# Small-head attentions on one NeuronCore: stacks of bf16 pieces through DRAM scratch, in whole rows

## What is computed

```python
x = x + _L0_attn_a_ref(_layernorm(x, axis=-1), ...)   # "norm": q and k normalised by head
x = x + _L0_ffn_ref(_layernorm(x, axis=-1), ...)      # six layers of window attention and FFN
x = x + _L0_attn_b_ref(_layernorm(x, axis=-1), ...)   # "latent": causal
x = x + _L0_ffn_ref(_layernorm(x, axis=-1), ...)
x = x + _L1_attn_a_ref(_layernorm(x, axis=-1), ...)   # linear attention
x = x + _L1_ffn_ref(_layernorm(x, axis=-1), ...)
x = x + _L1_attn_b_ref(_layernorm(x, axis=-1), ...)   # "plain": causal
x = x + _L1_ffn_ref(_layernorm(x, axis=-1), ...)

scores = jnp.einsum('bhsk,bhtk->bhst', Q, K) / jnp.sqrt(jnp.asarray(d_k, x.dtype))
scores = jnp.where(causal, scores, -jnp.inf)          # latent and plain
probs = jax.nn.softmax(scores, axis=-1)
attn = jnp.einsum('bhst,bhtk->bhsk', probs, V)
```

## Time and profile before

| | us |
|---|---|
| median of 3 executions | 4672.77 (4668.33 to 4675.03) |
| the profiled execution | 4673.36 |
| its span, first to last instruction | 4671.1 |
| norm attention, about | 65 to 392 |
| latent attention, about | 2100 to 2420 |
| plain attention, about | 4300 to 4620 |
| DVE, ACT, POOL busy | 3373.8, 2957.3, 2325.9 |

### The profile page before, as it was taken

The page is one execution under the profiler, slowest core; times in us unless marked ns, Lnnn a source line. Parts: engine busy times, 40 slices in busy tenths (PEclk is TensorE's granted clock), DMA queues, the critical chain, the costliest instruction groups (busy, mean ns, idle before and its releaser), DMA issues. The chain is left out here.

```text
span 4671.1 us, 129984 instructions
## 1 busy us (share of the span) xinstructions
PE 4231.0 (91%) x54074; PEld 2082.5 (45%) x54074; DVE 3373.8 (72%) x5180; ACT 2957.3 (63%) x7379; POOL 2325.9 (50%) x1448
## 2 busy tenths in 40 slices
PE   5897999999999999976879999999999999877698
PEld 2222555545455554532434545555555555433343
DVE  3673888888888888853648888888888888633463
ACT  2664777777777777752546777777777777643354
POOL 3101766666666666642007666666666666401200
PEclk8997999999999999986999999999999999988799
DMA  5212000000000000003210000000000000000320
GB/s 153 30 22 59 2 20 7 2 20 7 20 7 20 7 2 2 2 4 41 42 37 25 2 20 7 20 7 20 7 3 24 2 2 2 2 4 9 53 31 10
DMA packets 87862, 88.62 MB, mean 19 GB/s; under 512 B 36632, under 2 KB 79860, under 8 KB 83444
## 3 DMA queue, kind: packets, MB, share of 16 engines
q1 hardware_dynamic: 86420, 74.11, 7.7%
q10 hardware_dynamic: 864, 6.29, 0.3%
HBM read 44.13 MB, written 7.34 MB: 11 GB/s over the span
## 5 line engine op out<-in xcount | busy, mean ns | idle before, releaser
L423 POOL TENSOR_TENSOR ra<-ra,rb 128x1024 f32<-128x1024 f32 x384 | 926.9, 2414 | 348.0 <-DVE rb L725 347.9
L437 POOL TENSOR_TENSOR qkr<-ra,inv 128x1024 f32<-128x1024 f32 x384 | 731.0, 1904 | 612.8 <-ACT inv L677 609.1
L467 PE MATMUL ps<-wvo,xs 128*32 128x512 f32 x6144 | 825.1, 609 | 88.1 <-ACT vs L608 67.9
L501 PE MATMUL ps<-wq,xs 128*128 128x512 f32 x1536 | 751.7, 612 | 19.1 <-DMA wq<-in_L_ffn_Wqkv 18.4
L650 ACT ACTIVATE pr<-ps,neg 128x64 f32<-128x64 f32 x3072 | 667.8, 337 | 4.0 <-DVE neg L702 3.9
L608 ACT ACTIVATE vs<-ps 128x512 f32<-128x512 f32 x768 | 450.8, 587 | 251.7 <-PE ps L467 250.7
L1448 DVE TENSOR_REDUCE nm<-ps 128x1 f32<-128x512 f32 (+3 forms) x768 | 382.2, 549 | 244.3 <-PE ps L1257 243.2
L523 PEld LDWEIGHTS ps<-kt,qt 64*32 64x32 f32 x24576 | 359.6, 107 | 293.3 <-issue 289.5
L501 PEld LDWEIGHTS ps<-wq,xs 128*128 128x128 f32 x1536 | 275.0, 192 | 447.4 <-issue 355.9
L725 DVE TENSOR_TENSOR rb<-ps,rope 128x1024 f32<-128x1024 f32 x384 | 465.8, 1213 | 0.0
L722 DVE TENSOR_TENSOR ra<-ps,rope 128x1024 f32<-128x1024 f32 x384 | 451.3, 1175 | 18.6 <-ACT sq L624 11.5
(11 more groups left out here) (229 smaller groups left out, 6439.3 us busy)
## 6 DMA issues: line engine op xcount, KB each, us to landing
qs<-cut SPq DMA_DIRECT2D x216, 64.0 KB
ks<-cut SPq DMA_DIRECT2D x216, 64.0 KB
wq<-in_L_ffn_Wqkv SPq DMA_DIRECT2D x12, 1024.0 KB, 5.3
wvo<-wvo_scratch SPq DMA_DIRECT2D x12, 1024.0 KB, 5.0
wvo_scratch<-pt ACTq DMA_DIRECT2D x6, 1024.0 KB, 4.3
w<-in_L_ffn_W SPq DMA_DIRECT2D x12, 341.0 KB
pt<-in_L_ffn_Wqkv SPq DMA_DIRECT2D x6, 512.0 KB, 8.2
pt<-in_L_ffn_Wo SPq DMA_DIRECT2D x6, 512.0 KB, 7.7
```

Of the source, the lines that this page charges most:

```text
L423: pool.tensor_tensor(ra[:, m % 2, :, :], ra[:, m % 2, :, :], rb[:, :, :], ALU.add).then_inc(sum_done.sem, 1)
L437: pool.tensor_tensor(qkr[:, m % 2, :, :].rearrange("p s (h c) -> p (s h) c", c=HD), ra[:, m % 2, :, :].rearrange("p s (h c) -> p (s h) c", ...
L467: last = pe.matmul(VP[32 * j:32 * j + 32, :], xs[:, turn % 2, v * WIN:v * WIN + WIN], wvo[:, l % 2, j, :], start=True, stop=True)
L501: last = pe.matmul(PJ[:, qk, :], xs[:, turn % 2, t * P:t * P + P], wq[:, l % 2, at:at + 512], start=True, stop=True)
```

## The change

`cut` is no longer copied into the stacks directly. There is a scratch tensor in DRAM per attention, `pieces` (batch, piece, q or k, channel, token). `store_cut` (L1110 of the new kernel) stores each piece as soon as it is split, in three transfers of 256 KB a batch, counted by `cut_stored`. The channels of q and k are now ordered channel first over all 16 heads, so a channel's 16 heads are one contiguous run in `pieces`. `stack` (L1117 for `qs`, L1120 for `ks`) reads 24 rows of a stack at a time. For q they are the 8 channels of one piece, each repeated three times; for k they are the 8 channels of all three pieces. With all heads a row is 16 KB and a transfer 384 KB.

Batch 0 is read in 12 transfers of half the heads, right behind its stores. The other batches are read in 6 transfers, two each at 7, 9 and 11 heads from the start of the batch before, and their stores stand at 1. POOL's split of the next batch waits for `cut_stored` instead of `ld_low` and `ld_high`; `ld_high` is used for batch 0 alone. In the set-up of "norm", `gb` is loaded in 4 transfers instead of 8.

```diff
-    loads = 2 * PARTS * PARTS
+    loads = 2 * PARTS
+    SLOT = PARTS * SD
+    STACK_AT = (7, 9, 11)
+    pieces = nc.dram_tensor(f"{kind}_pieces", (BATCH, PARTS, 2, P, SEQ), BF16, kind="Internal").ap()
...
-                        for e in range(2):
-                            by_row = d[f"{n}_{name}"][:, None].to_broadcast([SD, SH // 2])
-                            sp.dma_start(gb[P // 2 * e:P // 2 * e + P // 2, col:col + 1], by_row, allow_slow_non_contiguous=True).then_inc(ld_w.sem, 16)
+                        by_row = d[f"{n}_{name}"][:, None].to_broadcast([SD, SH])
+                        sp.dma_start(gb[:, col:col + 1], by_row, allow_slow_non_contiguous=True).then_inc(ld_w.sem, 16)
...
-            def stacks(b, low):
-
-                heads = slice(0, SH // 2) if low else slice(SH // 2, SH)
-                half = slice(0, P // 2) if low else slice(P // 2, P)
-                done = ld_low if low else ld_high
-                for part_ in range(PARTS):
-                    sp.wait_ge(cut_done.sem, cut_done.at(5 * b + 2 * part_ + 1))
-                    for to, s, p, c in [(qs, 0, c // PARTS, c) for c in range(PARTS * PARTS)] + [(ks, 1, c % PARTS, c) for c in range(PARTS * PARTS)]:
-                        if p != part_:
-                            continue
-                        rows = slice(SD * c, SD * c + SD)
-                        sp.dma_start(to[rows, b % 2, heads, :], cut[half, p, s, :]).then_inc(done.sem, 16)
+            def store_cut(b, p):
+                sp.wait_ge(cut_done.sem, cut_done.at(5 * b + 2 * p + 1))
+                sp.dma_start(pieces[b, p].rearrange("s r t -> r s t"), cut[:, p, :, :]).then_inc(cut_stored.sem, 16)
+
+            def stack(b, s, p, heads, done):
+
+                rows = (qs, ks)[s][SLOT * p:SLOT * p + SLOT, b % 2, heads, :]
+                if s == 0:
+                    of_part = pieces[b, p, 0].rearrange("(c h) t -> c h t", c=SD)[:, heads, :].rearrange("c h t -> c (h t)")
+                    sp.dma_start(rows, of_part[:, None, :].to_broadcast([SD, PARTS, rows.shape[1] * SEQ])).then_inc(done.sem, 16)
+                else:
+                    all_parts = pieces[b, :, 1].rearrange("e (c h) t -> c e h t", c=SD)[:, :, heads, :].rearrange("c e h t -> c e (h t)")
+                    sp.dma_start(rows, all_parts).then_inc(done.sem, 16)
...
                 if (b := batch_at(k, 1)) is not None:
-                    if b >= 2:
-                        sp.wait_ge(st_mm.sem, st_mm.at(NP * (SH * (b - 2) + SH // 2)))
-                    stacks(b, True)
-                if (b := batch_at(k, 7)) is not None:
-                    if b >= 2:
-                        sp.wait_ge(st_mm.sem, st_mm.at(NP * SH * (b - 1)))
-                    stacks(b, False)
+                    for p in range(PARTS):
+                        store_cut(b, p)
+                    if b == 0:
+                        sp.wait_ge(cut_stored.sem, cut_stored.at(16 * PARTS))
+                        for heads, done in ((slice(0, SH // 2), ld_low), (slice(SH // 2, SH), ld_high)):
+                            for p in range(PARTS):
+                                stack(b, 0, p, heads, done)
+                                stack(b, 1, p, heads, done)
+                for p, at in enumerate(STACK_AT):
+                    if (b := batch_at(k, at)) is not None and b >= 1:
+                        if p == 0:
+                            sp.wait_ge(cut_stored.sem, cut_stored.at(16 * PARTS * (b + 1)))
+                            if b >= 2:
+                                sp.wait_ge(st_mm.sem, st_mm.at(NP * SH * (b - 1)))
+                        stack(b, 0, p, slice(0, SH), ld_low)
+                        stack(b, 1, p, slice(0, SH), ld_low)
...
                     if b:
-                        pool.wait_ge(ld_low.sem, ld_low.at(16 * loads * b))
-                        pool.wait_ge(ld_high.sem, ld_high.at(16 * loads * b))
+                        pool.wait_ge(cut_stored.sem, cut_stored.at(16 * PARTS * b))
```

More of the change, by code:

```diff
@@ L102, in constants @@
         "head_of_channel": np.kron(np.eye(SH), np.ones((SD, 1))).astype(np.float32),
-        "mean_of_8": np.kron(np.eye(2), np.kron(np.full((SD, SD), 1 / SD), np.eye(SH // 2))).astype(np.float32),
+        "mean_of_8": np.kron(np.full((SD, SD), 1 / SD), np.eye(SH)).astype(np.float32),
         "sum_rows": np.kron(np.eye(4), np.outer(np.arange(32) == SD, np.ones(32))).astype(np.float32),
@@ L949, in small_attention @@
     qk_normed, qk_ready, cut_done = ev("sa_qk_normed", "sa_qk_ready", "sa_cut_done")
-    ld_low, ld_high, *ld_m = ev("sa_ld_low", "sa_ld_high", "sa_ld_m_even", "sa_ld_m_odd")
+    cut_stored, ld_low, ld_high, *ld_m = ev("sa_cut_stored", "sa_ld_low", "sa_ld_high", "sa_ld_m_even", "sa_ld_m_odd")
     vw_turned, vw_made, vw_kept_act, vw_kept_dve, vw_out_act, vw_out_dve = ev(
@@ L1052, in _ @@
                         sp.dma_start(wo[l], d["L0_ffn_Wo"][l].rearrange("(k p) c -> p k c", p=P)).then_inc(ld_vw[l].sem, 16)
-            by_channel = lambda a: a.rearrange("p s (e c h) -> p s e h c", e=2, c=SD)
-            by_head = lambda a: a.rearrange("p s (e h c) -> p s e h c", e=2, c=SD)
-            n_ld = {"norm": 3 + 8 + 4, "latent": 7 + 4, "plain": 4}[kind]
+            by_channel = lambda a: a.rearrange("p s (c h) -> p s h c", c=SD)
+            by_head = lambda a: a.rearrange("p s (h c) -> p s h c", c=SD)
+            n_ld = {"norm": 3 + 4 + 4, "latent": 7 + 4, "plain": 4}[kind]
             @block.vector
@@ L1067, in _ @@
                     dve.tensor_tensor(by_channel(w[:, 0:2, :]), by_head(tmp[:, 0:2, :]),
-                                      mean.rearrange("p s (e h) -> p s e h", e=2)[:, :, :, :, None].to_broadcast([P, 2, 2, SH // 2, SD]), ALU.subtract).then_inc(prep_dve.sem, 1)
+                                      mean[:, :, :, None].to_broadcast([P, 2, SH, SD]), ALU.subtract).then_inc(prep_dve.sem, 1)
                     dve.tensor_copy(w[:, 2, :], tmp[:, 2, :])
@@ L1082, in _ @@
                     dve.wait_ge(prep_pe.sem, prep_pe.at(5))
-                    dve.tensor_copy(by_channel(w[:, 0:2, :]), ps[:, 0, 0:2 * P].rearrange("p (s e h c) -> p s e h c", s=2, e=2, c=SD))
+                    dve.tensor_copy(by_channel(w[:, 0:2, :]), ps[:, 0, 0:2 * P].rearrange("p (s h c) -> p s h c", s=2, c=SD))
                     dve.tensor_copy(w[:, 2, :], ps[:, 0, 2 * P:3 * P])
@@ L1247, in scores @@
                     pe.wait_ge(ld_low.sem, ld_low.at(16 * loads * (b + 1)))
-                if n_ == 0 and h == SH // 2:
-                    pe.wait_ge(ld_high.sem, ld_high.at(16 * loads * (b + 1)))
+                if n_ == 0 and h == SH // 2 and b == 0:
+                    pe.wait_ge(ld_high.sem, ld_high.at(16 * loads))
                 if i_ >= 3:
@@ L1518, in small_attention @@
     ones_set.past(1)
-    for e in (ld_low, ld_high):
-        e.past(16 * loads * BATCH)
+    ld_low.past(16 * loads * BATCH)
+    ld_high.past(16 * loads)
+    cut_stored.past(16 * PARTS * BATCH)
     for e in ld_m:
```

## The result

The changed kernel takes 4566.4 us (median of 4 executions, 4561.4 to 4575.7) against 4673.9 for the kernel before on the same chip, a ratio of 0.9774 (95% interval 0.9755 to 0.9792): 107.5 us less. The profiled execution took 4575.7 us with a span of 4573.4, at the upper end of its kind; the profiled one of before had 4671.1. The two spans that the rows come from differ by 97.7 us.

The account below looks back on a forecast made before the run. TensorE, busy 4231.0 of 4671.1 us, was held to lose 77.1 us waiting for late copies of row maxima; -77.1 + 2 + 1.4 + 2 - 12 - 1.5 = -85.2 from 4673.4 gave 4588 us, range 4564 to 4632.

Parts of the forecast that it names:

- Term 1: All three small-head attentions: TensorE's 11 waits for late copies of the row maxima go, -77.1 us.
- step (b): First maxima of a stage: GpSimd waits for stores alone, so the split comes earlier and the 21.41 us wait goes whole.
- Step (c): The other eight waits, behind or between blocks of 18 issues, go; at most two issues then stand ahead of maxima.
- step (d): Stack refill on the maxima's DMA rings: a pair of 384 KB reads takes 6.3 us; +2 us (0 to +8).
- rival A: The refill blocks the maxima, a pair taking near 7.75 us and the slow clock staying: 4630 us, chance 0.13.
- rival B: Loads run no faster than the stacks before, 63 GB/s, a pair taking 12.2 us: 4753 us, chance 0.04.
- Step (e): Stage starts: store and read back give head 0 its rows 20.4 us after the first split; plain stage +1.4 us.
- The set-up: Set-up of the attentions: four loads of `gb` instead of eight, -1.5 us (0 to -2.5).
- Step (f): Without the waits, later batches' preparation runs closer behind its producers on ScalarE, VectorE and GpSimd: +2 us (0 to +5).
- Term 2: Stretches at 1.2 GHz follow the waits in the attentions and shrink with them: -12 us (0 to -24).
- The marks: Signs to check: no maxima wait over 1 us, latent batches about 49, 55, 53, 46 us, clock near 1.00 in batches 1 and 2.

Follow-up runs that it names:

- e6: The kernel before with each block of 18 issues cut so that at most 6 stand ahead of maxima, rows still together: 4604.1 us.
- e9: The kernel before with one line changed, the 8 rows of each stack copy 9 partitions apart: 4594.8 us.
- e11: The kernel before with both small edits, copy rows 9 partitions apart and blocks of 18 issues cut in three: 4579.9 us.
- e1: The kernel before with two `cut` buffers in the latent and plain attentions: 4646.5 us.
- e3: The changed kernel with GpSimd's split of the next batch waiting again for the landed stacks, not the stores: 4573.7 us.
- e4: The changed kernel with each read of 24 rows cut into three of 8, so 18 reads a batch, still through DRAM: 4661.8 us.
- e7: The changed kernel without DRAM scratch: 18 SBUF-to-SBUF copies of 128 KB a batch, the 8 rows of each 9 partitions apart: 4559.6 us.
- e8: The changed kernel without DRAM scratch: 18 SBUF-to-SBUF copies of 128 KB a batch, the 8 rows of each next to each other: 4762.7 us.
- e2: The changed kernel with all six reads of a batch at 7 heads instead of two each at 7, 9 and 11: 4623.9 us.
- a0: The changed kernel run again unchanged, as reference for the first group of experiments: 4568.6 us, ratio 0.9776.
- e5: The kernel before with discarded matmuls filling some four fifths of TensorE's waits for late maxima: 4674.5 us.

## Why the prediction was right, and where it was not

The time, 4566.4 us, lies in the range (4564 to 4632) and 22 us under the forecast of 4588, just below the lower end of the forecast's own range (4568). The terms below go by the two profiled executions: there 97.7 us were saved where 85.2 were predicted, and the profiled execution of after was 9.3 us above its median.

**Term 1 (steps b and c), -77.1: measured -76.7.** All eleven waits for maxima fell under 1 us. The queue was rightly named: splitting the blocks alone takes 51 of the 77 us of waits (e6), quicker transfers alone 60.5 (e9), and both all (e11). One link of step (b) was not needed for the maxima. The early release of `cut` is worth 28 us in the kernel before (e1) and nothing measurable in the changed one (e3), where the split comes 7 us later and the maxima are in time all the same. What step (b) and (c) do not contain, though the change doesn't work without it (e4), is that a transfer of 24 neighbouring rows is spread over more of SBUF than one of 8; e7 and e8 show that placement alone does this. Step (c) is also wrong that at most two issues stand ahead of maxima: four reads stand ahead of the third, as step (d) has it, and at this rate they do no harm.

**Step (d), a pair of reads in 6.3 us, +2 for the refill: right.** Two reads of 384 KB were through in 5.7 us (2182.9 to 2188.6), and the refill stalls nothing: the longest landing of maxima is 4.5 us. That 6.3 came so near is in part luck. It was priced from 16 KB packets of another queue (q8), at 1.06 us each, and rival A was held unlikely because of "16 KB rows instead of 1 KB pieces". The size of the packets doesn't set the time: the same 16 KB took 0.90 us with 24 rows a read and 2.1 with 8. With 8 rows a read (e4) the margin is gone, as rival B's mechanism has it: transfers at some 60 GB/s gave 93 us back. B's price of 159 us was too high for this form, since TensorE waited 55.8 us for maxima and 22.2 for the first stacks; but e8, slower than the kernel before by 1.85%, is that rival in the flesh. Rival A's mechanism shows in e2: three pairs ahead of the second maxima instead of one, and 37 us of waits are back.

**Step (e), the round trip: right.** Plain attention, first split to first score: 20.4 us predicted, 20.3 measured (4258.93 to 4279.25), with a visible wait of 2.83 us. In the latent attention the trip was hidden but for 0.6.

**The set-up, -1.5: measured -2.2.** The first score of the norm attention came at 88.0 instead of 90.2. The last load of the set-up is issued at 31.5 to 31.7 us in every kernel with four loads of `gb` and at 33.8 to 34.3 in those with eight; the first score scatters more (86.1 in a0).

**Step (f), +2 for producers seen more closely: somewhat too small.** TensorE's idle time in the loops, without the waits for maxima, rose by 6.3 us (4.5 in a0), where (d) and (f) had 4 together. Waits for ScalarE's `pt` are as before (10.0 and 9.4 us in the latent attention). Those for DVE's `nm` went from 6.2 to 9.1 us in the norm attention (6.5 in a0) and from 2.8 to 5.1 in the plain one (4.2 in a0).

**Term 2, the clock, -12 (0 to -24): the term that was too small.** In the profiled executions the loops shrank by 91.8 us, 15.1 more than the waits; in the repeated one by 100.2, 23 more. Windows over the three loops part this; their sums before (90.2 to 389.9, 2138.8 to 2405.8, 4344.1 to 4601.4 us) and after (88.0 to 374.9, 2117.6 to 2340.3, 4279.2 to 4501.8):

```profile
sum 824.00, PE 690.89 PEld 285.12 DVE 499.47 ACT 426.62 POOL 78.52; mean PE 230.30 PEld 95.04 DVE 166.49 ACT 142.21 POOL 26.17
sum 732.20, PE 669.49 PEld 277.09 DVE 499.40 ACT 424.29 POOL 76.53; mean PE 223.16 PEld 92.36 DVE 166.47 ACT 141.43 POOL 25.51
```

For as many matmuls (1113, 1620 and 1616 in both) TensorE is busy 21.4 us less, and 27.9 less in a0 (662.97). Where the clock is 1.00 in both kernels, in latent batch 3, its busy time is the same (43.85 and 43.86 us). So the 21.4 are the clock's, and 21.4 less the 6.3 of idle time above makes the 15.1. The step that failed is my argument that the clock "can cost nothing too". It compared latent and plain batch 2 with each other, 53.2 and 53.5 us after deducting their waits. Both were stretched alike: in the changed kernel they take 50.2 and 49.9 us. What a batch costs at full clock was to be had only from a batch without late waits, and there was none of that kind in the trace. The windows of e9 show the price directly, 5.6 us beyond a wait of 3.3. Across the table's kernels, e5 left out, the loops less their waits grow by 0.26 us for each microsecond at 1.2 GHz (a straight line through 13 executions). For the 95.5 us that went, this gives 25 us, a correlation over kernels that differ in other things too, but in accord with the busy times. So the clock gave 21 to 28 us, at the upper end of my range, where I had booked 12.

**The marks.** I expected latent batches of about 49, 55, 53 and 46 us and read 43.2, 59.9, 50.2 and 45.6. Batch 0 lost more of its slow clock than I allowed. Batches 1 and 2 are at 1.00 as I expected but for latent batch 1 (0.94, or 7 us at 1.2 GHz), where no wait for maxima stands and the cause is open. Batch 1 is longer by my own error. The row statistics and projections of batch 3 run at heads 22 to 29, inside batch 1, and batch 2 carries no such preparation; the windows above show it in DVE's and ScalarE's instructions, 98 and 69 against 94 and 60. I had treated the two as alike in work, and taken for slow clock what batch 1 costs more.

**The rest of the 97.7 us.** Waits 76.7, other loop time 15.1, set-up 2.2, starts -1.7 (0.4 and 1.3 longer) leave 5.4. As much as that and more, 6.5, lies between the end of the norm attention and the first split of the latent one, where the kernels do the same work: 1727.5 us in the profiled execution of before, 1721.0 in that of after, and 1722 to 1727 in those of the experiments. That is one execution against another, and no part of the forecast.

## What to carry to other kernels

Before transfers are merged or sent through DRAM, look at the partitions that each one writes: eight rows 9 partitions apart moved at 172 GB/s, eight neighbours at 58, and one changed line gave two thirds of what the whole rewrite gave. A small urgent copy behind bulk loads waits for the issues ahead of it plus the bytes in flight, so shortening either can be enough, and their gains do not add. A wait of TensorE costs more than it shows, here 5.6 us beyond one of 3.3, so price it by a batch that has none.

## What the runs showed that was not expected

- The partition placement of a transfer's rows changes the time of a 1 KB packet from 47 to 152 ns.
- SyncE's issue of a transfer takes 0.61 to 0.65 us for 64 or 128 KB in rows of 1 KB and for 384 KB in 24 rows of 16 KB, but 0.30 us for the 128 KB of e4 in 8 rows of 16 KB. It is not the bytes that set it. In e1 it took 1.06 each (3.17 for three) while the block before was still moving.
- DVE's small operations on the maxima are held while GpSimd splits. The plain attention of the changed kernel, GpSimd at 4314.34 beside DVE's operations as their durations in ns, min/median/max (start at 4314.4; the same operation without GpSimd took 0.28 us, as the second shows), and the wait that it gave TensorE:

```profile
4314.34 2.13 POOL L1176 TENSOR_TENSOR x<-x,cut 128x1024 f32<-128x1024 f32 x1
L1471 DVE TENSOR_TENSOR m<-mf,mcut x1: 2247/2247/2247, 4314.4 to 4314.4; 16x128 f32<-16x128 f32 x1
L1475 DVE TENSOR_TENSOR m<-m,mcut x1: 280/280/280, 4317.7 to 4317.7; 16x128 f32<-16x128 f32 x1
4318.86 0.28 PE L1267 MATMUL ps<-cmask,ident 128*128 128x128 bf16 x1 [2.43 <-DVE nm L1459]
```

The casts of the maxima beside GpSimd's casts are held too, 851 and 998 ns, where the same casts take 0.21 us undisturbed. The Trainium skill ("SBUF — State Buffer", terms, shared port pair) says that DVE and GpSimd lock a pair of ports for a whole instruction; the 2247 ns against 280 agree. What this costs depends on where the split falls. The longest wait for `nm` in the plain attention is 2.4 us in the changed kernel and 6.9 in e11, whose split is held for the loads and falls wholly on the five operations (4289.85 to 4296.8 us, which take 1.3 us when undisturbed). So in a kernel without the early release the later split can cost what the maxima no longer do.
